# Loads of x and swaps of kv issued ahead of the round trip of the softmax sums, in a fused attention and FFN kernel

## What is computed

```python
q_big = einsum('bshk,hkq->bshq', layernorm(x) @ Wq.T, w_kc_q)
kv_rope = kv_c * cos + rotate_half(kv_c) * sin
q_r = einsum('bshq,hqr->bhsr', q_big, W_qr);  k_r = einsum('bld,hdr->bhlr', kv_rope, W_kr)
attn = softmax(einsum('bhsr,bhlr->bhsl', q_r, k_r), axis=-1)
ctx_c = einsum('bhsl,bld->bhsd', attn, kv_rope)
x = x + einsum('bhsd,hkd->bshk', ctx_c, w_kc_kv).reshape(b, s, H * K) @ Wo.T
x = x + bitlinear(gelu(bitlinear(layernorm(x), w1)), w2)   # inputs in 8 bits, weights in -1, 0, 1
```

## Time and profile before

| | |
|---|---|
| time of the runs shown, median (lowest to highest) | 399.08 us (397.65 to 399.17) |
| the profiled execution | 399.17 us |
| its span, from the first to the last instruction | 397.3 us |
| mean granted clock of TensorE | 0.996 of full speed |
| busy: TensorE | 380.2 us, 96% |
| busy: VectorE, ScalarE, GpSimd | 313.4, 267.2, 270.2 us (79, 67, 68%) |
| transfers | 48.11 MB, mean 121 GB/s |
| the two broadcasts into rb | 64 issues of 256 KB, median 3.9 us to landing |
| loads of x | 8 issues of 512 KB, median 5.9 us |
| swaps of kv | 8 issues of 128 KB, median 5.8 us |

### The profile page before, as it was taken

One profiled execution on the slowest core, in us unless ns is written; L12 is line 12 of the kernel. 1 busy time (PEld: TensorE's weight loads), 2 busy tenths in 40 slices (PEclk: granted clock), 3 DMA queues, 4 the chain that ended last, 5 costly groups with the idle time before them and its releaser, 6 DMA issues. The chain is left out here.

```text
span 397.3 us, 9040 instructions
## 1 busy us (share of the span) xinstructions
PE 380.2 (96%) x2938; PEld 290.9 (73%) x2954; DVE 313.4 (79%) x664; ACT 267.2 (67%) x487; POOL 270.2 (68%) x410
## 2 busy tenths in 40 slices
PE   8999999999999999999999999999999999899796
PEld 7778557777766877888777878787878787576575
DVE  0454987788999898988888888888888889896684
ACT  1245383344678777686868786868686868868693
POOL 2127737855676787878786868687777767685784
PEclk9999999999999999999999999999999999999899
DMA  8994345556323224234243443425252434466243
GB/s 218 371 374 177 102 135 139 147 146 151 80 69 82 69 73 123 65 86 118 83 122 83 95 111 83 119 70 135 70 132 72 124 79 112 107 88 159 63 108 107
DMA packets 62862, 48.11 MB, mean 121 GB/s; under 512 B 47712, under 2 KB 53216, under 8 KB 62432
## 3 DMA queue, kind: packets, MB, share of 16 engines
q1 hardware_dynamic: 62208, 44.00, 42.2%
q10 hardware_dynamic: 608, 3.54, 2.5%
HBM read 31.92 MB, written 4.46 MB: 92 GB/s over the span
## 5 line engine op out<-in xcount | busy, mean ns | idle before, releaser
L470 POOL TENSOR_TENSOR cl<-cr,ch 128x512 fp32r<-128x512 f32 x60 | 76.4, 1294 | 69.1 <-ACT ch L667 69.1
L651 ACT ACTIVATE qf<-ps 128x512 f32<-128x512 f32 x64 | 38.3, 598 | 73.1 <-PE ps L891 73.1
L889 PE MATMUL ps<-xh,ah 128*128 128x256 f32 x256 | 75.7, 296 | 0.7 <-ACT g L693 0.3
L891 PE MATMUL ps<-xh,al 128*128 128x256 f32 x256 | 71.9, 281 | 0.0
L890 PE MATMUL ps<-xl,ah 128*128 128x256 f32 x256 | 71.9, 281 | 0.0
L955 PE MATMUL hps<-bh,ch 128*128 128x256 f32 x224 | 66.6, 297 | 0.0
L957 PE MATMUL hps<-bh,cl 128*128 128x256 f32 x224 | 63.1, 282 | 0.0
L956 PE MATMUL hps<-bl,ch 128*128 128x256 f32 x224 | 63.0, 281 | 0.0
L889 PEld LDWEIGHTS ps<-xh,ah 128*128 128x128 f32 x256 | 48.1, 188 | 17.8 <-issue 16.0
L667 ACT ACTIVATE ch<-cr 128x512 fp32r<-128x512 f32 x64 | 39.2, 632 | 16.7 <-DVE cr L1268 16.7
L1235 DVE TRANSPOSE_TENSOR_REDUCE red<-hps 128x16 f32<-128x512 f32 x64 | 41.8, 691 | 8.8 <-PE hps L908 8.4
(11 more groups left out here) (157 smaller groups left out, 878.2 us busy)
## 6 DMA issues: line engine op xcount, KB each, us to landing
rb<-rinv_d SPq DMA_DIRECT2D x64, 256.0 KB, 3.9
xs<-x SPq DMA_DIRECT2D x8, 512.0 KB, 5.9
out<-xs SPq DMA_DIRECT2D x32, 128.0 KB, 3.7
wq_s<-wq SPq DMA_DIRECT2D x2, 1024.0 KB, 14.5
w_s<-w_t SPq DMA_DIRECT2D x2, 1024.0 KB, 6.6
wo_s<-wo_t ACTq DMA_DIRECT2D x1, 2048.0 KB, 10.5
wk_a<-wk_t SPq DMA_DIRECT2D x2, 512.0 KB, 7.4
kvs<-kvn SPq DMA_DIRECT2D x8, 128.0 KB, 5.8
```

Of the source, the lines that this page charges most:

```text
L470: pool.tensor_tensor(cl[:, u % 2, :, b * S:(b + 1) * S], cr[:, :, b * S:(b + 1) * S], ch[:, u % 2, :, b * S:(b + 1) * S].bitcast(F32), ALU ...
L889: pe.matmul(o, ah[:, c, cols], xh[:, k % 2, c, :], start=(c == 0), stop=False)
L891: m = pe.matmul(o, al[:, c, cols], xh[:, k % 2, c, :], start=False, stop=(c == KC - 1))
```

## The change

In SyncE's list the x load and, in iterations 3 to 5, the wait for `rope_done` with the two swaps go ahead of the stores and broadcasts of the inverse sums. The text of the change moves the calls of `turn_g(n - 9)`, `rinv_rows` and `rinv_spread` down; since x loads and swaps end with iteration 6, and `turn_g(n - 9)` begins with iteration 9, the order is a different one in iterations 1 to 6 only. In iteration 0 there is no tile n-1. No other engine's list changes, and no wait is added or taken away.

```diff
                     if n % 2 and tile(n - 10):
                         turn_g(n - 10)
-                    if n % 2 and tile(n - 9):
-                        turn_g(n - 9)
-                    if tile(n - 1):
-                        rinv_rows(n - 1)
-                        rinv_spread(n - 1)
                     if n == 0:
                         sp.dma_start(w2_s[:, :, :], w2_t.rearrange("(a p) n -> p a n", p=P)).then_inc(sem["w2_loaded"], 16)
                     if 1 <= n < 7:
                         load_x(n + 1)
                     if n in (3, 4, 5):
                         sp.wait_ge(sem["rope_done"], n - 2)
                         swap_kv(n - 2)
+                    if n % 2 and tile(n - 9):
+                        turn_g(n - 9)
+                    if tile(n - 1):
+                        rinv_rows(n - 1)
+                        rinv_spread(n - 1)
                     if tile(n - 11):
                         store(n - 11)
```

## The result

In runs taken in turn on the same chip the changed kernel took 400.57 us (median of 11, 399.61 to 403.94) and the kernel before 397.86 us (median of 11). The ratio is 1.0081, with a 95% interval of 1.0055 to 1.0105: 3.2 us slower, from 2.2 to 4.2. It takes in all 38 executions of the changed kernel, whose median is 401.1, and is therefore a little more than the 2.7 us between the two medians of 11. The prediction was 401.6 us from 399.17, a ratio of 1.006 (2.45 us).

What follows compares the result with a forecast made beforehand. TensorE, without slack behind the changed stretch, was taken to bound the kernel. Terms for iterations 2, 3, 4 and 6, 1.65 + 0 + 0.3 + 0.5 = 2.45 us, on 399.17 gave 401.6 us; range 399.0 to 404.2.

Steps and rivals of the forecast that it cites:

- What bounds it: TensorE, without slack behind the changed stretch: delay before 100 us reaches the end one to one, later rows shift by a constant.
- Queueing: SyncE's DMA queue, iterations 1 to 6: a store completes only after the 512 or 768 KB queued ahead of it.
- The rival of stores that slip past: Stores not held back, only issue time counts: 0.35 us reaches TensorE in iteration 2, total 399.2 to 399.5; chance 0.2.
- Iteration 2: Broadcasts into rb 2.05 us later, division 1.9 us late, minus 0.25 us hidden: 1.65 us lost by TensorE.
- the 0.25 us that I took as hidden on VectorE: Iteration 2: VectorE's idle time at 56.64 hides at most 0.25 us of a late division.
- the estimate of 3.2 us: Landing time of x by 2.0 us + bytes/436 GB/s; would make iteration 2's term 0.75 us, total about 400.4.
- Iteration 3: Broadcasts about 2 us later, but 1.5 us in hand and the iteration before 1.65 us longer: 0.
- Iterations 4 and 5: Broadcasts 6.35 us behind the shift; division of iteration 4 0.85 us late, 0.3 us lost; nothing put in iteration 5.
- the slow drain: Rival: kvs swaps take 5.2 us, stores of iterations 3 to 5 complete 1.15 us later, total 404.8; chance 0.15.
- Iteration 6: turn_x behind late broadcasts delays the shift transfer, whose reader has no slack, by 0.5 us; late division falls beside this wait.
- the prediction's second rival: Not slower: x behind the broadcasts was the harm; 0.4 us gained, 398.8, down to 397; chance 0.04.
- Iteration 7: No term of its own in the sum; TensorE's start there was to be late by 2.5 us.

Runs made afterwards that it cites:

- first x alone: Kernel before with only the x load of iteration 1 moved ahead of the stores of the inverse sums; ratio 1.0035 (1.0016 to 1.0054).
- all but the first: Changed kernel with iteration 1 as before: x loads of iterations 2 to 6 and swaps of 3 to 5 ahead; ratio 1.0054 against the kernel before.
- before profiled again: The kernel before, unchanged, profiled a second time; ratio 0.9997 (0.9960 to 1.0035).
- x alone: Kernel before with only the x loads of iterations 1 to 6 ahead of the stores, the swaps behind as before; ratio 1.0063 (1.0043 to 1.0083).
- last x alone: Kernel before with only the x load of iteration 6 (part 7) ahead of the stores; ratio 1.0011 (0.9977 to 1.0045).

## Why the prediction was right, and where not

**What bounds it.** TensorE's delay was to reach the end one to one, and nothing of it was won back: 8 to 31 takes 240.0 to 240.7 us in every version. But the rows behind 110 us were to be shifted by a constant, and in the changed kernel they were not: it has the longest of these, 240.72, which is 0.6 to 0.7 us over the two profiles of before. 0.36 us of it lie between iterations 16 and 17; I have no cause for that, and no second profile of it.

**Queueing** was the step on which the forecast stood, with one sample behind it. Every version with 512 KB or more ahead shows it, one of them across two queues. The rival of stores that slip past fell: the broadcasts went out 5.1 us behind the shift, where it had 3.9 (50.8 - 46.94).

**Iteration 2:** predicted 1.65 us; measured 10.21 against 8.44 to 8.89, that is 1.3 to 1.8. The step was right and its terms were not. x alone was taken as 4.1 us and took 3.7 (3.5 in "first x alone"); the stores landed 0.3 us behind it and not 0.1. So the broadcasts were 1.86 us late and not 2.05, and the division 1.8 and not 1.9, counted from the row maxima of iteration 1. Against that, the 0.25 us that I took as hidden on VectorE was eaten by `wfactor` (L1347), which took 1.26 us there and 0.94 in before, first before and then after:

```profile
56.90 0.94 DVE L1347 TENSOR_SCALAR wfactor<-wtotal 128x2 f32<-128x2 f32 x1
```

```profile
58.76 1.26 DVE L1347 TENSOR_SCALAR wfactor<-wtotal 128x2 f32<-128x2 f32 x1
```

The two errors, near 0.1 us less and 0.25 more, partly offset one another. For x the estimate of 3.2 us worked out from the Trainium skill (page DMA: Bandwidth & Descriptors, the section on the SWDGE path, whose fit is for transfers that GpSimd issues and not SyncE), which I set aside for the trace, was 0.5 off where my value was 0.4 off; in "first x alone" (3.5 us) it is nearer than mine.

**Iteration 3:** predicted 0, measured 0. The reason was half wrong: I counted the lengthened iteration before it as cover, but "all but the first", without that cover, lost nothing either.

**Iterations 4 and 5:** the broadcasts 6.35 us behind the shift were predicted, 6.4 to 6.5 measured. That it fits is in part luck: for x alone the same sum gives 1.2 + 4.1 + 0.1 = 5.4 us where 5.1 was measured, and the swaps, put at 0.95, added 1.3 to 1.4. The loss, 0.3 and 0, came out as 0.25 to 0.3 and 0. The swaps landed 3.8 to 4.0 us after issue in iterations 3 to 5 of the changed kernel, here iteration 5, so the slow drain did not come:

```profile
DMA to landing us min/median/max: 3.9/3.9/4.0
```

The swapped parts are first read by the contexts of tile 8, which TensorE does in iteration 9 and not in 8 as the prediction has it; nothing hangs on it.

**Iteration 6:** predicted 0.5 us beyond what before already lost. The mechanism is the one named: counted from the row maxima of iteration 6, `turn_x` behind the late broadcasts begins 0.66 us and the shift transfer behind it goes out 0.61 us later than in before. Yet 6 to 7 is only 0.07 us longer, because TensorE had the shift 2.3 us after its issue (94.21 to 96.53), where in before it had it after 2.9 (91.18 to 94.12). There x and the swaps of iteration 5 were issued just ahead of it, and the last of them landed at 93.1. Such a gain at the shift stands in the prediction's second rival, but not in its sum. That x and the swaps cause the 0.6 us fits the finding on the stores and was not tested by itself.

Against before profiled again, which does not wait for this shift, and against the other profiles without x ahead that take 9.28 to 9.33 us, the changed kernel (10.02) and x alone (9.93) take 0.6 to 0.75 us more, but "all but the first" (9.58), whose list is the same from iteration 2 on, only 0.3. The scatter at this place is as large as the term (up to 0.65 us), so the term is likely and not shown, and here the single profile of before misled me.

**Iteration 7:** predicted nothing, measured 0.59. This is the term that the sum put at nothing. I had asked what the late rb of iteration 5 does in iteration 6, and found it beside the wait for the shift; I did not carry the same sum one further. The last x delays the broadcasts of iteration 6 to 5.35 us behind a shift that is late itself, and the division of iteration 7 waits 0.89 us, as its twin in "last x alone" waits 0.84. The broadcasts' landing, and then VectorE:

```profile
DMA to landing us min/median/max: 3.6/3.8/4.0
```

```profile
104.37 1.29 DVE L1268 TENSOR_TENSOR cr<-ps,rb 128x512 f32<-128x512 f32 x2 [0.89 <-issue]
105.58 0.68 DVE L331 TENSOR_TENSOR xl<-ps,xh 128x512 fp32r<-128x512 f32 x1
```

The second broadcast, issued near 100.3, landed at 104.3, as the division began. TensorE's FFN matmul waits for `x_lo` behind the division (its row stands in the section on the result). Four versions have this x ahead and take 10.66 to 11.07 us from 7 to 8; all others take 10.12 to 10.17.

**The sum:** 1.65 + 0 + 0.3 + 0 + 0.5 + 0 = 2.45 us predicted for iterations 2 to 7. Against the two profiles of before the same distances give 1.3 to 1.8, 0, 0.25 to 0.3, 0, 0.1 to 0.7 and 0.6, together 2.7 or 2.9; with the 0.6 to 0.7 behind iteration 8 that have no cause here, the changed kernel is 3.3 or 3.6 us longer from 1 to 31, and 3.2 timed. So the loss was forecast 0.75 us too small, within the interval of the measurement. That the time itself came so close, 401.6 against 401.1 for all executions, is partly luck: the sum started from 399.17 us, and in the runs taken in turn the kernel before stood at 397.86, 1.3 us lower.

## What to carry over

A small transfer that someone waits for should not be issued behind a large one that nobody waits for: here it waited until the large one's bytes had landed, and the one run that used another queue found no way past them. Before moving an issue, look up how long the reader of each transfer behind it has in hand, iteration by iteration; here the one iteration with none paid about half the price, and iterations 3 to 5 paid nothing for broadcasts that were 1.4 us late. And a wait seen in one profiled execution may be that execution's own: a second profile of the same kernel settles it for the price of one run.

## What the runs showed of the hardware

A load of 128 KB of x with only the two shift transfers ahead of it landed after 2.1 us, 512 KB after 3.5 to 3.7, and of two loads of 512 KB the second 4.5 us after its issue. Stores of 4 KB behind 128 KB took 1.4 to 1.8 us, behind 512 KB 2.8 to 3.1, behind 1 MB 3.7 to 3.8. A load on ScalarE's queue held back small transfers on SyncE's, both the stores (2.6 and 3.4 us, the second 1.2 us beyond the landing of the load) and the shift that was issued in the same moment (0.89 us of wait). And the clock granted to TensorE was 0.83 over 10 us of the tail in both profiled executions of before, after TensorE had paused for 2.8 and 2.5 us, and 1.00 in that of the changed kernel, after a pause of 1.9 us: enough to hide half of the difference in the spans.
